# Attention steps of a two-layer kernel: half a value product and half a projection piece in every step

## What is computed

```python
qkv = xs @ Wqkv + bqkv                       # 1024 pixels, 512 channels -> q, k, v
scores = jnp.einsum('bhqd,bhkd->bhqk', q, k) / jnp.sqrt(64)     # 8 heads of 64
attn = jax.nn.softmax(scores, axis=-1)
out = jnp.einsum('bhqk,bhkd->bhqd', attn, v)
out = out @ Wout + bout
x = x + out                                  # layer 0; then layer 1 on windows of 8 x 8 pixels
```

## Time and profile before

| | |
|---|---|
| median of 3 runs | 3008.57 us (3002.29 to 3011.41) |
| the profiled execution, its own time | 3005.0 us |
| its span, first to last instruction | 3003.2 us |
| TensorE (PE) busy | 2771.4 us, 92% |
| VectorE (DVE) busy | 2201.0 us, 73% |
| ScalarE (ACT) busy | 1665.8 us, 55% |
| steps 1 to 22 of attention, eight images together | 1091.87 us |
| mean granted TensorE clock | 0.971 |

### The profile page before, as it was taken

How to read it: one execution, slowest core, us unless ns; L and a number is a source line. 1 busy time by engine, 2 the same in 40 slices (tenths; PEclk the granted TensorE clock), 3 DMA queues, 4 the chain that set the end, 5 groups by cost and what they waited for, 6 DMA issues and landing times.

```text
span 3003.2 us, 60746 instructions
## 1 busy us (share of the span) xinstructions
PE 2771.4 (92%) x25208; PEld 1948.6 (65%) x25208; DVE 2201.0 (73%) x2934; ACT 1665.8 (55%) x2429; POOL 197.3 (7%) x157
## 2 busy tenths in 40 slices
PE   6999799999999999999999999999999999998858
PEld 5666576756667577665776667765677756765434
DVE  5676577687875877868877778768787588775856
ACT  2653466375653755636665556636566375554625
POOL 0000001000200002000020000200020000200300
PEclk9999899999999999999999999999999999998968
DMA  5233012421233112340224311232123311105040
GB/s 202 66 74 107 36 43 76 135 81 45 59 95 130 48 54 60 89 174 8 65 59 134 113 43 39 80 130 86 45 52 101 131 48 54 38 12 175 13 110 29
DMA packets 149602, 235.85 MB, mean 79 GB/s; under 512 B 78609, under 2 KB 97556, under 8 KB 145460
## 3 DMA queue, kind: packets, MB, share of 16 engines
q1 hardware_dynamic: 148468, 219.39, 23.7%
q10 hardware_dynamic: 864, 12.58, 1.2%
HBM read 177.08 MB, written 54.84 MB: 77 GB/s over the span
## 4 chain that ended last, share of the span: by engine, by line
PE 73%; DVE 12%; ACT 5%; DMA 4%; issue 4%; another core or an unknown queue 1%; SPq 0%; DVEq 0%; POOL 0%; ACTq 0%
PE banks L708 12%; PE banks L648 10%; PE banks L677 9%; PE banks L695 8%; PE banks L638 6%; PE banks L894 5%; PE banks L750 5%; PE banks L904 4%; PE banks L896 4%; PE banks L895 4%; DMA recips_dram<-recips 3%; DVE neg_max L1432 3%; DVE exps_turned L1443 2%; ACT exps L1111 2%; PE banks L867 2%
## 5 line engine op out<-in xcount | busy, mean ns | idle before, releaser
L1432 DVE TENSOR_REDUCE neg_max<-banks 128x1 f32<-128x1024 f32 x512 | 601.8, 1217 | 88.8 <-PE banks L677 86.0
L1111 ACT ACTIVATE exps<-banks,neg_max 128x1024 f32<-128x1024 f32 x512 | 566.8, 1113 | 47.4 <-DVE neg_max L1432 46.3
L1123 ACT ACTIVATE exps_turned<-banks 128x1024 f32<-128x1024 f32 x256 | 262.3, 1025 | 553.2 <-PE banks L695 544.9
L1443 DVE COPY exps_turned<-banks 128x1024 f32<-128x1024 f32 x256 | 313.2, 1223 | 262.3 <-PE banks L695 247.5
L677 PE MATMUL banks<-qk_halves 64*128 64x512 f32 x3072 | 432.9, 412 | 60.7 <-ACT exps L1111 39.6
L708 PE MATMUL banks<-exps_turned,values 128*64 128x256 f32 x4096 | 481.1, 384 | 0.8 <-issue 0.8
L695 PEld LDWEIGHTS banks<-ident,exps 64*128 64x128 f32 x8192 | 311.5, 139 | 199.1 <-issue 171.3
L695 PE MATMUL banks<-ident,exps 64*128 64x64 f32 x8192 | 366.6, 228 | 31.4 <-DVE exps_turned L1443 27.3
L708 PEld LDWEIGHTS banks<-exps_turned,values 128*64 128x64 f32 x4096 | 280.3, 137 | 138.8 <-issue 5.1
L677 PEld LDWEIGHTS banks<-qk_halves 64*128 64x128 f32 x3072 | 292.4, 189 | 109.9 <-issue 75.8
L1613 DVE SCALAR_TENSOR_TENSOR qk_halves<-banks,qk_halves 128x1024 fp32r<-128x1024 f32 x256 | 302.0, 1219 | 67.2 <-ACT qk_halves L1160 66.9
(11 more groups left out here) (187 smaller groups left out, 3388.9 us busy)
## 6 DMA issues: line engine op xcount, KB each, us to landing
wqk_ring<-wqk_split SPq DMA_DIRECT2D x62, 512.0 KB
wo_halves<-wo_split_dram SPq DMA_DIRECT2D x8, 2048.0 KB, 7.8
exps_turned<-in_x SPq DMA_DIRECT2D x32, 512.0 KB, 5.6
x_dram<-exps SPq DMA_DIRECT2D x32, 512.0 KB, 2.6
exps_turned<-x_dram SPq DMA_DIRECT2D x32, 512.0 KB, 6.0
out<-exps_turned SPq DMA_DIRECT2D x32, 512.0 KB, 2.6
recips_b<-recips_dram SPq DMA_DIRECT2D x240, 64.0 KB, 3.4
x_image<-in_x SPq DMA_DIRECT2D x14, 1024.0 KB, 7.0
```

Source lines behind the costliest of these rows:

```text
L1111: freed(act.activation(PB[:, 2 * h + n % 2], slot(("s", m, i)), ACT.Exp, bias=NM[:, m:m + 1], accum_out=SS[:, m:m + 1]), ("s", m, i))
L1432: dve.tensor_reduce(NM[:, m:m + 1], slot(("s", m, i)), AX.X, ALU.max, negate=True).then_inc(mx, 1)
L1443: dve.tensor_copy(PT[:, n // 2 % 2, 1, :, P * j:P * j + P].rearrange("p k (r q) -> p k r q", r=2), TB.rearrange("p r (k q) -> p k r q", k= ...
```

## The change

Every step from 2 to 21 gets half a value product and half a piece. Even steps take the first half of the value product, and behind it the second half of `piece(n)`; odd steps take the second half of the value product, and behind it the first half of `piece(n + 1)`. A piece is thus complete one step later than before, and its high and low parts move one step later on ScalarE and VectorE as well. Piece 0 stays whole in step 0. With it move: `offsets` and `tanh` (step 4 to 5), `log` and the sample points (5 to 6), `hats` (6 to 9), `group_sums` and `group_variance` (22 to 23); SyncE gets a wait on `off_done`, since the buffer that the first sample of the next image lands in also feeds `offsets`.

```diff
             def load_sample(c, k):
                 wait_after(sp, xs_done, 8 * (k - 1) + c - 1)
+                if c == 0:
+                    wait_after(sp, off_done, k - 1)
...
-            def piece(n, i):
+            def piece(n, half, i):
                 p, which = piece_of(n)
                 w, c = which // 2, 512 * (which % 2)
-                pe.wait_ge(wq_in[w], 16 * (PAIRS * i + p))
-                wait_after(pe, piece_free, (i * 3 + p - 1) * PIECES + which)
-                if n == 6 and i:
-                    pe.wait_ge(off_done, i)
-                project_halves(MB, WQ[:, w], c, range(CT)).then_inc(piece_full, 1)
+                if half == 0:
+                    pe.wait_ge(wq_in[w], 16 * (PAIRS * i + p))
+                    wait_after(pe, piece_free, (i * 3 + p - 1) * PIECES + which)
+                    if n == 6 and i:
+                        pe.wait_ge(off_done, i)
+                mm = project_halves(MB, WQ[:, w], c, range(2 * half, 2 * half + 2))
+                if half == 1:
+                    mm.then_inc(piece_full, 1)
...
                     if n == 0:
-                        piece(0, i)
-                    if n >= 2 and n % 2 == 0:
-                        value_product(n // 2 - 1, 0, i)
-                    if (2 <= n < 22 and n % 2 == 0) or (n > 22 and n % 2):
-                        value_product(n // 2 - 1, 1, i)
+                        for half in range(2):
+                            piece(0, half, i)
+                    if i and n == 5:
+                        offsets(i - 1)
+                    if i + 1 < B and n == 23:
+                        pe.wait_ge(piece_free, (i + 1) * MAXES)
+                        group_sums(2 * i + 2, GSM)
+                    if n >= 2:
+                        value_product(n // 2 - 1, n % 2, i)
                     if piece_of(n + 1):
-                        piece(n + 1, i)
+                        piece(n + 1, 0, i)
+                    if n and piece_of(n):
+                        piece(n, 1, i)
...
                     copy_turned(n, i)
+                    if i and n == 5:
+                        tanh(i - 1)
...
-                    if (2 <= n < 22 and n % 2 == 0) or (n > 22 and n % 2):
+                    if n > 2 and n % 2:
                         keep_output(n // 2 - 1, i)
...
-                    if piece_of(n + 1):
-                        high_piece(n + 1, i)
+                    if n and piece_of(n):
+                        high_piece(n, i)
...
-                    if i and n == 5:
+                    if i and n == 6:
                         log(i - 1)
...
-                    if piece_of(n + 1):
-                        low_piece(n + 1, i)
+                    if n and piece_of(n):
+                        low_piece(n, i)
```

More of the change, by code:

```diff
@@ L1009, in _ @@
                     turn(n, 1, i)
-                    if i and n == 4:
-                        offsets(i - 1)
                     if i and n == 23:
@@ L1019, in _ @@
                         sampled_keys(i - 1)
-                    if i + 1 < B and n == 22:
-                        pe.wait_ge(piece_free, (i + 1) * MAXES)
-                        group_sums(2 * i + 2, GSM)
                     if i and n == 27:
@@ L1269, in _ @@
                         high_piece(0, i)
-                    if piece_of(n + 1):
-                        high_piece(n + 1, i)
+                    if n and piece_of(n):
+                        high_piece(n, i)
                     if i and n == 3:
                         gelu(i - 1)
-                    if i and n == 4:
-                        tanh(i - 1)
-                    if i and n == 5:
+                    if i and n == 6:
                         log(i - 1)
@@ L1755, in _ @@
                         convolve_sum(n // 2 + 2, multiplied)
-                    if i and n == 5:
+                    if i and n == 6:
                         sample_points(i - 1)
                         log_inputs(i - 1)
-                    if i and n == 6:
+                    if i and n == 9:
                         hats(i - 1)
@@ L1764, in _ @@
                         log_row((n - 8) // 2, (n - 8) % 2, i - 1)
+                    if i + 1 < B and n == 23:
+                        group_variance(2 * i + 2, GSM)
                     copy_turned(n, i)
-                    if i + 1 < B and n == 22:
-                        group_variance(2 * i + 2, GSM)
                     if i and n == 26:
```

## The result

The changed kernel is slower: a median of 3094.6 us (3093.5 to 3100.5, four runs) against 3005.4 us (2989.5 to 3011.4, four runs) of the kernel before, a ratio of 1.0307 with a 95% interval of 1.0283 to 1.033. The forecast was 3117, in a range from 3070 to 3155. The profiled execution after has a time of 3095.25 us and a span of 3093.4 us, 90 us more than before.

What follows compares the result with a forecast made beforehand. TensorE bounds the kernel, busy 2771 of 3003 us. To 3005 us came cuts 30, pair waits 54, clock 18, `offsets` 4.5, `group_sums` 2, reloads with steps 1 and 22 3: 112, so 3117, range 3070 to 3155.

Steps and rivals of the forecast that it cites:

- a cut pair of steps: Two neighbouring regular steps, each with half a value product and half a piece: about 12.44 us instead of 12.08.
- all cuts: Ten value products and 11 pieces newly cut per image, at 0.16 and 0.20 us each: 30 us for eight images.
- waits of a new pair: TensorE's scores after pieces 6, 14 and 22 wait for VectorE's low part: 24 times 2.26 us, 54 us.
- the clock behind them: TensorE's granted clock falls after the 24 new waits, at 0.75 us each: 18 us, bounds 0 and 66.
- `offsets`: Moved to step 5, where nothing covers its 0.64 us: 7 times, 4.5 us.
- waits of before that went: TensorE's 30.0 us of waits in steps 1 to 22; the sum counted none of them as won back.
- The rival of free cuts: Next block's weights load during the last matmuls, so cutting costs nothing: 82 us added, 3087; chance 0.08.
- The rival of the covered wait: Another chain, exponentials to score buffers, holds a pair's first scores as long, so neither 54 nor 18 is paid: 3045; chance 0.08.
- slack in step 7: One in three new waits falls in a step with room, so the clock's cost was set at 0.75 us each.
- The rival with 66: Every new wait is followed by a low clock as in the longest case, 66 us instead of 18: 3165; chance 0.14.
- Faster: Evenly dealt steps win back most of the 30 us of TensorE waits, at best 2975 us; chance 0.10.
- the reloads: Exp table reloads, now in steps 4 and 7 with less TensorE work: 0.3 us an image, within a 3 us term.

Runs made afterwards that it cites:

- early-weights kernel: The kernel of the pieces dealt one step earlier, with SyncE issuing the next pair's weights ahead of the reciprocals' transfers: 3015.9 us, 1.0051 to the kernel before.
- the quarters: The kernel of the pieces dealt one step earlier, with value-product and piece halves cut again and laid alternately in steps 2 to 21: 3072.0 us, 1.0231 to the kernel before.
- the low part first: The changed kernel, with VectorE making the low part before the copy of the second turned head in steps 6, 14 and 22: 3050.9 us, 1.0172 to the kernel before.
- two copies: The changed kernel, with VectorE making the copy of the second turned head twice in steps 6, 14 and 22: 3141.8 us, 1.0465 to the kernel before.
- the pieces dealt one step earlier: The changed kernel, with piece 2 whole in step 1, later pieces a step earlier and moved layer 1 work back in its old steps: 3037.7 us, 1.012 to the kernel before.

## Why the prediction was right, point by point

| term | predicted | measured |
|---|---|---|
| a cut pair of steps | +0.36 | +0.38 |
| all cuts | 30 | 28 (busy time, steps 1 to 22) |
| waits of a new pair | 54 | 24 x 2.49 = 60, of them 4 another wait |
| the clock behind them | 18 | 167.7 - 149.7 = 18 |
| `offsets` | 4.5 | 7 x 0.30 = 2 |
| waits of before that went | 0 | -11 (odd steps 3 to 21) |
| all terms | 112 | 91 (profiles), 89 (medians) |

- **The cuts.** Regular pairs of 12.44 were expected, 12.46 came, without a wait in them. The rival of free cuts falls, by the regular pair of the early-weights kernel (12.46) and by the quarters (+0.35 a step). The 28 us of the table are the busy time with the low part first, which has all the cuts of the change and none of its low clock: its windows of steps 1 to 22 have

```profile
sum 1147.89, PE 1090.06; mean PE 136.26
```

against 1061.8 before. The prediction read the standstill of the weight loads too widely: in the trace of before they stand for 0.39 behind a value product and 0.35 behind a piece (medians), but for 0.07 where a value product or a piece begins behind a turn. The change that the new order adds, from a value product to a piece, has the 0.39, as in this row of after:

```profile
1554.98 0.19 PEld L650 LDWEIGHTS banks<-x_hi,wqk_ring 128*128 128x128 f32 x1 [0.39 <-issue]
```

The Trainium skill, TensorEngine Tiling (Array Packing), Key Properties, which the prediction weighed, has a change of tiling mode drain TensorE; the quarters, which add only such changes, agree.
- **The pair wait.** Place, cause and number were right. Steps 6 and 22 came out 2.26 and 2.28 longer than a regular 6.23, as worked out. Step 14 is 2.85 longer: 0.54 of that is another wait, of the first turn for a late copy, told below. The rival of the covered wait falls: the step follows the wait's length one to one, down and up.
- **The clock.** 18 us were put down, from six cases in the trace of before; against the kernel in which it never fell it is 18. That the number fits so well is in part luck. The six cases (steps of 5.56 twice, 6.82, 7.07, 7.09 and 8.33) average 1.2 a wait and not the 1.0 of the prediction, and the reduction to 0.75 was for slack in step 7; but step 7 lost as much as the others (6.3 us, against 6.1 in step 15 and 5.6 in step 23). It came out at 0.75 a wait because the clock fell behind 15 of the 24, at 1.2 us a fall. The rival with 66 falls, and even with waits of 3.4 us and a low clock behind 23 of 24 the price was 183.8 - 149.7 = 34.
- **Faster.** The dealing alone, with both of its new waits out of the way, is still slower (1.0032 at the lower end). This rival's idea, that dealt steps give room to late copies, is true in size of some 10 us and not of the 30 that it hoped for. The waits that went were not in the steps with a value product, where it looked for them, but in the short ones with a piece.
- **What was too high.** The sum is 21 us above the 91. The cuts are not the reason, since TensorE's busy time grew by nearly what was put down for them. The term that was mis-sized is one that the sum put at nothing: it left the 30 us of waits of the kernel before as they are, and the prediction's first paragraph says that the unevenness of the steps costs nothing. Eleven of these 30 us were the price of the short odd steps and went (17.9 before; 6.8 in the early-weights kernel, 6.9 after). Another 7 us are steps 0 and 24 to 29, which the sum left alone; 4.4 of them are the single long step in the profiled execution of before. How the small rest divides between the reloads, `offsets` and steps 1 and 22 is not shown.

## What to carry to other kernels

On an engine that is nearly full in every step, dealing the work evenly wins back only the waits of the short steps (11 us here), and every further cut between blocks of different kinds has a price (28 us here) that the trace shows beforehand in blocks of other lengths. What a cut delays is its block's completion: look for the in-order wait that comes next behind it, and lay the other queue's order (here copy and low part on VectorE) so that the awaited result comes first. A step need not be as long as its neighbour; it must only not be shorter than the chain of engines that it runs through, or the time taken out of it is paid in the other one.

## What the runs showed of the hardware

**The clock's answer is steep.** Waits of 1.0 us on average let the granted clock stay at 1.00 in 24 of 24 cases, waits of 2.1 us lowered it to 1.2 GHz for a while in 15 of 24, waits of 3.4 us in 23 of 24. Each fall cost 18 / 15 = 1.2 us after and 34 / 23 = 1.5 with two copies. Halving the wait removed all of it. The length of a wait does not decide alone: with the pieces dealt one step earlier the clock fell behind waits for weights of 1.83 and 2.81 us, but stayed at 1.00 behind this one of 3.11, as the window from there on shows:

```profile
2294.72 0.50 PE L650 MATMUL banks<-x_hi,wqk_ring 128*128 128x512 f32 x1 [3.11 <-DMA wqk_ring<-wqk_split]
```

```profile
2294.72:2300.95 6.23, 6.23 (x66) 4.25 (x66) 3.67 (x5) 1.77 (x2) 0.00 (x0) 1.00 0.55 108
```

**VectorE beside GpSimd.** In steps 12 to 15 of all images but the first GpSimd scales and shifts the `pixels` of the image before. Timeline after, in steps 12 to 14:

```profile
1561.21 10.41 POOL L621 TENSOR_TENSOR pixels<-pixels,ln_w 128x512 f32<-128x512 f32 x8 [144.38 <-DVE neg_max L1438]
...
1562.24 0.41 DVE L1571 COPY attended<-log_parts 64x512 bf16<-64x512 bf16 x1
...
1567.71 1.36 DVE L1470 TENSOR_TENSOR attended<-attended,recips_b 128x256 f32<-128x256 f32 x1
...
1568.99 1.49 DVE L1571 COPY attended<-log_parts 64x512 bf16<-64x512 bf16 x1
...
1570.40 1.21 DVE L1449 COPY exps_turned<-banks 128x1024 f32<-128x1024 f32 x1
...
1571.76 0.71 PE L697 MATMUL banks<-ident,exps 64*128 64x64 f32 x16 [0.54 <-DVE exps_turned L1449]
```

Two operations of VectorE whose operands all lie in the on-chip memory that GpSimd uses too (SBUF) take 1.36 and 1.49 us; elsewhere they take 0.40 and 0.41 or less, and the copy out of the banks keeps its 1.2. The GpSimd instructions that ran when the two began, each by itself:

```profile
1567.49 1.29 POOL L621 TENSOR_TENSOR pixels<-pixels,ln_w 128x512 f32<-128x512 f32 x1
```

```profile
1568.75 1.45 POOL L621 TENSOR_TENSOR pixels<-pixels,ln_w 128x512 f32<-128x512 f32 x1
```

They ended at 1568.78 and 1570.20, and the two slow operations 0.29 and 0.28 later (1567.71 + 1.36 = 1569.07 and 1568.99 + 1.49 = 1570.48). So each took about what the GpSimd instruction had left, and then some 0.3 of its own. The Trainium skill, SBUF — State Buffer, Who interferes with whom, describes an exclusive lock of the port pair that the two engines share, in which the later one stands until the other's instruction has ended; the two slow rows agree. The first copy began 0.27 before the end of a GpSimd instruction (1561.21 + 1.30 = 1562.51) and took its usual 0.41; no stand is visible there, and why is not shown. The trace of before has the same slow operations, in two different steps. After the change both fall into one step, and the copy behind them is late enough to hold a turn for 0.54: in step 14 of seven images (the first has no such work beside it), some 4 us.
